# The analysis convolution as 7x7 output blocks with patches as stationary operands, and weight preparation between its products

## The reference

```
x2  = relu(x)                                          # (8,16,56,56)
sub = conv(x2 as (128,1,56,56), f_ana (9,1,9,9), 'SAME')
x3  = concat([sub as 144 channels, x2 (16 channels)])  # (8,56,56,160) tokens
for l, shift in enumerate((0, 3)):
    x3 = x3 + proj(attention(layernorm(x3), windows 7x7, shift))
    x3 = x3 + gelu(layernorm(x3) @ w1 + b1) @ w2 + b2
x3  = x3 @ linw + linb                                 # then a synthesis convolution, a 1x1 convolution
```

## Time and profile before

| what | value |
|---|---|
| median of 3 runs | 3282.6 us (3275.31 to 3290.77) |
| the profiled execution | 3282.26 us, span of its profile 3280.7 us |
| busy, share of the span: PE, PEld | 95%, 86% |
| busy: DVE, ACT, POOL | 67%, 51%, 25% |
| mean granted clock of TensorE | 0.976 |

### The profile page before, as it was taken

The page is one execution under the profiler, slowest core; times in us unless marked ns, Lnnn a source line. Parts: engine busy times, 40 slices in busy tenths (PEclk is TensorE's granted clock), DMA queues, the critical chain, the costliest instruction groups (busy, mean ns, idle before and its releaser), DMA issues. The chain is left out here.

```text
span 3280.7 us, 104199 instructions
## 1 busy us (share of the span) xinstructions
PE 3128.1 (95%) x40530; PEld 2817.2 (86%) x40530; DVE 2190.6 (67%) x6717; ACT 1676.8 (51%) x4073; POOL 832.6 (25%) x1464
## 2 busy tenths in 40 slices
PE   7996999999999999999999999999999999999589
PEld 6784888888888888888888888888888888888589
DVE  1113677777777777777777777777777777777332
ACT  1111566666666666666665555555555556555221
POOL 4400122222222222222222222223232222232110
PEclk9997799999999999999999999999999999999799
DMA  4421011111111111111211111111111111111385
GB/s 88 119 71 51 20 38 37 37 37 37 37 37 37 37 37 37 37 37 37 56 42 39 37 32 36 26 36 37 37 37 31 36 26 37 37 37 26 60 147 89
DMA packets 246679, 148.39 MB, mean 45 GB/s; under 512 B 31729, under 2 KB 246068, under 8 KB 246586
## 3 DMA queue, kind: packets, MB, share of 16 engines
q1 hardware_dynamic: 244882, 146.95, 19.4%
q0 software_dynamic: 1728, 0.48, 0.1%
HBM read 96.74 MB, written 52.50 MB: 45 GB/s over the span
## 5 line engine op out<-in xcount | busy, mean ns | idle before, releaser
L1457 PE MATMUL rm<-w,ht 128*112 128x160 f32 x4480 | 681.0, 301 | 0.0
L1457 PEld LDWEIGHTS rm<-w,ht 128*112 128x112 f32 x4480 | 609.7, 177 | 5.8 <-ACT ht L1034 0.2
L944 POOL TENSOR_TENSOR rs<-ln_tmp,mhalf 112x4 f32<-112x4 f32 (+1 forms) x128 | 119.1, 930 | 1624.4 <-DVE ln_tmp L1116 1624.3
L1034 ACT ACTIVATE ht<-rm 128x448 f32<-128x448 f32 (+1 forms) x640 | 318.6, 498 | 193.8 <-PE rm L118 193.8
L118 PE MATMUL rm<-z2t_hi,w_hi 128*128 128x448 f32 (+1 forms) x640 | 257.5, 402 | 4.8 <-DVE z2t_rest L1226 3.3
L999 ACT ACTIVATE vb<-ra 113x320 f32<-113x320 f32 x256 | 112.9, 441 | 281.1 <-PE ra L118 279.6
L910 POOL TENSOR_TENSOR z<-z,one 112x448 f32<-112x448 f32 (+2 forms) x192 | 131.3, 684 | 354.1 <-DVE z L1120 354.1
L118 PE MATMUL rm<-z2t_rest,w_rest 98*128 98x448 f32 (+1 forms) x640 | 220.0, 344 | 0.0
L118 PE MATMUL rm<-z2t_hi,w_lo 128*128 128x448 f32 (+1 forms) x640 | 219.0, 342 | 0.0
L118 PE MATMUL rm<-z2t_lo,w_hi 128*128 128x448 f32 (+1 forms) x640 | 218.5, 341 | 0.0
L1165 DVE TENSOR_TENSOR sc<-so,tabs 113x490 f32<-113x490 f32 x256 | 171.3, 669 | 59.4 <-PE so L1403 46.9
(11 more groups left out here) (247 smaller groups left out, 9147.6 us busy)
## 6 DMA issues: line engine op xcount, KB each, us to landing
xa<-xs SPq DMA_DIRECT2D x128, 245.0 KB
xr<-xs SPq DMA_DIRECT2D x128, 245.0 KB
xs<-a_tok SPq DMA_DIRECT2D x8, 1960.0 KB, 9.5
xs<-xo SPq DMA_DIRECT2D x64, 245.0 KB
ys<-yz SPq DMA_DIRECT2D x64, 245.0 KB
c_y<-ys SPq DMA_DIRECT2D x48, 260.0 KB
c_y<-ys SPq DMA_DIRECT2D x16, 280.0 KB
c_taps<-in_f_syn SPq DMA_DIRECT2D x24, 126.0 KB, 5.3
```

The source lines that it names most:

```text
L944: gp.tensor_tensor(rs[1][:, t0:t0 + nt], ln_tmp[1][5][:, t0:t0 + nt], mhalf[:, 0:nt], ALU.pow).then_inc(s_pow, 1)
L1034: act_(ht[:, f * SN + t0 * TT:f * SN + (t0 + nt) * TT], bank_m(i, lm, use)[:, 0:nt * TT], ACT.Gelu_apprx_tanh).then_inc(m_freed(i, lm, use ...
L1457: last = mm(bank_m(i, lm, use)[0:TT, t * DIM:(t + 1) * DIM], ht[:, c:c + TT], keep.w["w2", lm][:, f * DIM:(f + 1) * DIM], start=(f == 0), ...
```

## The change

The convolution is laid out anew. The host hands over x padded to 64x64, two images of a pair side by side for each channel, and the filters as one table (`spread_taps`) of 15x15 rows by 490 columns (10 outputs by 7x7 positions, the tenth being the identity). A group `g` is 8 channels of a pair (there are 8 groups). `load_group` brings 128 partitions (8 channels x 2 images x 8 rows of windows) by 15x64 pixels. ScalarE's `relu` cuts them into eight 15x15 patches (`a_win`, 128x1800, one buffer). TensorE turns the patches in four steps `q` (`turn`: 4 transposes of 128x120 or 128x105), ScalarE and VectorE write the high and low parts with patches sorted by channel (`patch_out`, inner stride 8 elements), and for each channel TensorE adds 6 products (2 halves of the 225 patch elements by 3 combinations) in which the patches of 128 windows are the stationary operand and the table of 490 columns moves. That makes 384 products for 64 outputs. `output` copies 128x490 to the token tile, which now holds windows on partitions (inner stride 160 elements), ScalarE the even channels, VectorE the odd ones. The relu is part of the same output.

A pair's tokens are stored by 7 transfers with runs of 1120 elements, when its two groups are through. The last pair's store is issued in `phase_b`, behind its first loads. The token tile of that pair lives on through `phase_b`.

The weight preparation is cut in 13 uses of two PSUM banks (`USES`), one behind every second product of channels from number 26 on (`PREP_AT`). SP issues gains first, then raw weights, and lands each weight's own semaphore, for which GpSimd waits one by one. Bias rows are now the last two rows of `raw_c`, and their split is done by VectorE. The loop over images is unrolled on all engines.

```diff
@@ build
+        with ExitStack() as early:
+            late = LastPair(nc, early, xs0)
+            phase_a(nc, keep, late, x, f_ana, ...)
+            phase_b(nc, keep, late, xs0, xs1, ys)
...
@@ phase_a, sync engine
+            load_group(0)
+            for h in range(2):
+                for oy in range(WIN):
+                    sp.dma_start(view(tok[1], 0, PART[h], h * ON + oy * OXN, [[1, OXN]]),
+                                 dram(f_ana.tensor, (ROW0[h] - oy + WIN - 1) * (PR * OXN), [[OXN, PART[h]], [1, OXN]])
+                                 ).then_inc(s_taps[h], 16)
+            load_group(1)
+            sp.wait_ge(s_win, 1)
+            load_group(2)
...
+            for g in range(3, NG_A + 2):
+                if 3 < g < NG_A:
+                    sp.wait_ge(s_win, g - 1)
+                    load_group(g)
+                pair = (g - 3) // 2
+                if g % 2 == 0 and pair < B // 2 - 1:
+                    for n in range(4):
+                        sp.wait_ge(s_free[n], (pair + 1) * (C // 4))
+                    late.store_pair(sp, pair, tok[pair % 2], s_store[pair % 2])
...
@@ phase_a, scalar engine
+            def relu(g):
+                act.wait_ge(s_nat[g % 2], 16 * (g // 2 + 1))
+                reach(act, s_turn, 4 * g)
+                nc.scalar.activation(view(win, 0, 128, 0, [[PR * PR, WPR], [PR, PR], [1, PR]]),
+                                     view(nat[g % 2], 0, 128, 0, [[WIN, WPR], [PW, PR], [1, PR]]), ACT.Relu).then_inc(s_win, 1)
...
+            for g in range(NG_A):
+                for c in range(0, CG, 2):
+                    n = g * CG + c
+                    output(n)
+                    if g + 1 < NG_A and c < 6:
+                        patch_out(g + 1, c // 2)
+                    if c == 4:
+                        if g + 1 < NG_A:
+                            patch_out(g + 1, 3)
+                        if g + 2 < NG_A:
+                            relu(g + 2)
+                    if PREP_AT.get(n - 2) in ON_ACT:
+                        prep(PREP_AT[n - 2])
...
@@ phase_a, vector engine
+            for g in range(NG_A):
+                for c in range(1, CG, 2):
+                    n = g * CG + c
+                    if g + 1 < NG_A:
+                        patch_out(g + 1, c // 2)
+                    output(n)
...
@@ phase_a, tensor engine
+            def turn(g, q):
+                h, bank = q // 2, turn_ps[q % 2]
+                reach(pe, s_win, g + 1)
+                reach(pe, s_plo, 4 * g + q - 1)
...
+            def conv(g, c):
+                n = g * CG + c
+                if c == 0:
+                    pe.wait_ge(s_plo, 4 * (g + 1))
+                reach(pe, s_free[n % 4], n // 4)
+                cols = slice(c * 128, (c + 1) * 128)
...
+                    for p, b in ((patch_hi, band_hi), (patch_lo, band_hi), (patch_hi, band_lo)):
+                        last = nc.tensor.matmul(conv_ps[n % 4][:, 0:ON], p[g % 2][h][:, cols], b[h][:],
+                                                start=(k == 0), stop=(k == 5))
...
+            for g in range(NG_A):
+                for c in range(CG):
+                    conv(g, c)
+                    if g + 1 < NG_A and c in TURN_AT:
+                        turn(g + 1, TURN_AT.index(c))
+                    if g * CG + c in PREP_AT:
+                        prep(PREP_AT[g * CG + c])
...
@@ phase_b, sync engine
             load(xr, s_xr, 0, 0)
+            late.store_pair(sp, B // 2 - 1, late.tok, late.s_store)
             sp.wait_ge(s_norm[0], 1)
```

More of the change, by code:

```diff
@@ L57 @@
 FT = MLP // 128
-PADF = W - FS // 2 - 1
-FROW = 112
+PR, PW, WPR = WIN + FS - 1, H + FS - 1, W // WIN
+CG = C // 2
+ROW0 = (0, 8)
+PART = (8 * PR, 7 * PR)
+OXN = (K + 1) * WIN
+ON = WIN * OXN
+TURN_AT = [0, 2, 4, 5]
+PREP_FIRST = 26
 ZW = 128 + CR
@@ new lines, in band, with patch_out @@
+            def band(h):
+                act.wait_ge(s_taps[h], 16 * WIN)
+                nc.scalar.activation(band_hi[h][:], taps(h), ACT.Copy).then_inc(s_bhi, 1)
+            def patch_out(g, q):
+                act.wait_ge(s_turn, 4 * g + q + 1)
+                if g >= 2 and q == 0:
+                    last = CG * (g - 1) - 1
+                    act.wait_ge(s_conv[last % 4], last // 4 + 1)
+                nc.scalar.activation(patch(patch_hi, g, q), turned(g, q), ACT.Copy).then_inc(s_phi, 1)
@@ new lines, in output, with prep @@
+            def output(n):
+                act.wait_ge(s_conv[n % 4], n // 4 + 1)
+                tok_room(act, n)
+                nc.scalar.activation(tokens(n), sums(n), ACT.Copy).then_inc(s_free[n % 4], 1)
+            def prep(use):
+                act.wait_ge(s_pfull, USES.index(use) + 1)
+                p = prep_bank(use)
+                if use == "w2T0":
+                    last = nc.scalar.activation(w2t_a[:, 0:4 * 128], p[:, 0:4 * 128], ACT.Copy)
+                elif use == "w2T1":
+                    nc.scalar.activation(w2t_a[:, 4 * 128:MLP], p[:, 0:128], ACT.Copy)
+                    last = nc.scalar.activation(w2t_c[0:REST, 4 * 128:MLP], p[0:REST, 128:256], ACT.Copy)
+                else:
+                    last = nc.scalar.activation(w2t_c[0:REST, 0:4 * 128], p[0:REST, 0:4 * 128], ACT.Copy)
+                last.then_inc(s_pact, 1)
@@ L490, in _ @@
-            body(0, 0)
-            body(0, 1)
-            with dve.Fori(1, B // 2) as pair:
-                for u in range(2):
-                    body(pair, u)
-            n = 0
+            v = nc.vector
+            count = 0
             def step(ins):
-                nonlocal n
-                n += 1
+                nonlocal count
+                count += 1
                 ins.then_inc(s_prep, 1)
-                dve.wait_ge(s_prep, n)
-            dve.wait_ge(s_small, SMALL)
-            dve.wait_ge(s_bps, 1)
@@ L634, in _ @@
-            last.then_inc(s_fold, 1)
-def phase_b(nc, keep, xs0, xs1, ys):
+            def turn(g, q):
+                h, bank = q // 2, turn_ps[q % 2]
+                reach(pe, s_win, g + 1)
+                reach(pe, s_plo, 4 * g + q - 1)
+                for w in range(4):
+                    off = (4 * (q % 2) + w) * PR * PR + ROW0[h] * PR
+                    last = nc.tensor.transpose(bank[0:PART[h], w * 128:(w + 1) * 128], win[:, off:off + PART[h]], keep.ident[:])
+                last.then_inc(s_turn, 1)
@@ L638, in phase_b @@
+            pe.wait_ge(s_pool, 1)
+            for q in range(4):
+                turn(0, q)
+            for g in range(NG_A):
[5 more added lines that the diff above has]
+                        prep(PREP_AT[g * CG + c])
+def phase_b(nc, keep, late, xs0, xs1, ys):
     with ExitStack() as ctx:
```

540 lines of the change are left out of this document (242 added, 298 removed).

## The result

The changed kernel took 3136.3 us in the median of 4 runs (3129.97 to 3140.15), against 3282.2 us (3275.31 to 3290.77) for the kernel before on the same chip. The ratio is 0.9553, with a 95% interval of 0.9538 to 0.9569. The forecast was 3127 us, with a range of 3106 to 3156.

What follows compares the result with a forecast made beforehand. TensorE was taken to bound phase a: 15.2 + 2.0 + 85.2 + 12.2 + 20.1 + 4.2 + 7.2 + 2.0 + 1.3 = 149.4 us, where 303.95 stood. So 3282.3 - 154.6 = 3127.7, say 3127 us; range 3106 to 3156.

Steps and rivals of the forecast that it cites:

- Phase a is TensorE's: Phase a: TensorE as the bound with small stalls, 3115 to 3138 us, given 0.60.
- The products at 0.222 us: Convolution on TensorE: 384 products of 490 columns at 0.222 us each, together 85.2 us.
- Rival (b): Phase a: ScalarE and VectorE set the pace, at 1.4 us per strided operation; 3149 us, chance 0.12.
- Rival (d): Phase a evacuation: slower than before, ScalarE's strided operations 4.2 us each; about 3330 us at 5 us each, chance 0.02.
- The start: Phase a's beginning: loads, relu, transposes and splits put the first product at 15.2 us, where it stood at 9.4.
- The slow stretch behind it: TensorE's first products: some 11 at the lower clock, 0.41 instead of 0.22 us, costing 2.0 us.
- Group bubbles: Between groups: the next group's first product waits for VectorE's low part, 0.6 us in each of 7 groups, 4.2 us.
- That is a wait of 7.2 us: Group 3: TensorE waits 7.2 us for group 4, issued at 58.6 us behind SP's weight list; lower end 1.4 us.
- VectorE's and ScalarE's parts of it are to lie under later products: Weight preparation: these engines' 15.5 us are hidden under products, since groups 3 and 4 stay under TensorE's time.
- The preparation at 20.1 us: Weight preparation on TensorE, moved between products: 20.1 us at full clock, in place of 33.4 us.
- Stores, group 5's load, GpSimd: Phase a: pair stores of 13.9 us and group 5's load all hidden; GpSimd ends near 80 us.
- Its own signs: Profile checks: product spacing 0.22 us, first near 15, one group 3 wait of 1 to 8, phase b loads near 150.

Runs made afterwards that it cites:

- Experiment 4: Changed kernel with output copies written in runs of 7 instead of steps of 160 elements, tokens in wrong order: 3137.0 us, ratio 0.9558.
- Experiment 5: Changed kernel with four products per channel in place of six, leaving out patches' high part with table's low part: 3125.5 us, ratio 0.9526.
- Experiment 1: Changed kernel with the loads of groups 4 and 5 issued among the raw weights, not behind all weights: 3134.6 us, ratio 0.9551.
- Experiment 2: Changed kernel with ScalarE's weight preparation ahead of the patches and relu of the same step, not behind them: 3131.8 us, ratio 0.9543.
- experiment 3: Changed kernel with all weight preparation behind the last product of the convolution, as before the change: 3144.6 us, ratio 0.9586.
- experiment 6: Changed kernel with the last pair's store issued and waited for in phase a, ahead of phase b's loads: 3150.1 us, ratio 0.9599.
- experiment 9: The changed kernel itself, unchanged, run again in a later sitting: 3139.4 us, ratio 0.9566.
- 8: Experiment 7's kernel with pair 0's store issued right behind group 5's load and preparation from product 36 on: 3127.0 us, ratio 0.9532.
- experiment 7: Changed kernel with groups 4 and 5 loaded among raw weights, ScalarE's preparation ahead of its patches, preparation from product 30 on: 3120.1 us, ratio 0.9507.

## Why the prediction was right, and what it missed

**Phase a is TensorE's.** The products at 0.222 us held to the digit, and so did 0.41 us at the lower level of the clock. Rival (b) wanted 1.4 us for each strided operation, and none shows more than 1.18. Experiment 4 adds that with outputs at 0.58 us the kernel is no faster. Experiment 5 says how near the chain over ScalarE and VectorE was: of 3.55 us less in a group's products 1.3 turned into waiting. Rival (d) would have wanted four times the price that the rows show.

**The start** was put at 15.2 us and is 16.05. The slow stretch behind it was put at 2.0 us, and group 0 takes 15.28 us to the next group's first product where the others take 13.15, so 2.1 more.

**Group bubbles** were put at 0.6 us in each of 7 groups, 4.2 us, and measured 0.25 to 0.48 where they occur, 2.1 us in all. That the patches cost 1.18 us and not 1.05 did not show. Against that a group's own work took 12.7 us, not 12.4. Each change from transposes to products costs about 0.1 us, which the sum had not. The two about cancel.

**"That is a wait of 7.2 us"** is the mis-sized term. It measured 10.13: TensorE came 1.7 us later than said (59.24), and the relu ended 4.6 us later (69.31). The forecast issued group 4 at 58.6 us, and it was at 62.82. SP began with the weights 0.5 us later than said (9.56), and 3.7 us lie in the list itself, which took 52.7 us beside group 3's load where the earlier trace rows gave 49.0. It has single issues of 2.55, 2.00 and 4.26 us, as the list before had of other sizes. By comparison with their like the held issues come to some 9.0 us here, where the prediction counted 5.8 before. Why they were held no run shows. The prediction counted such held issues as possible savings at the lower end, and not as a cost that could grow. Experiment 1 confirms the cause: with the load moved up, the wait is gone. The wait's length isn't firm either. The same list ended in the other runs such that group 4 was issued between 62.23 and 65.58 us.

**"VectorE's and ScalarE's parts of it are to lie under later products"** is the step that failed. VectorE's part did lie there. The engines' busy times left room for ScalarE's too, and the order on ScalarE did not. A bank was freed 1.8 us late, and the low clock behind it took about 3.4 us more (7.94 us at 0.57). Experiment 2 removed both, 5.7 us. The prediction compared sums of busy time by group, and had not followed the queue of one engine at the places where another waits for it.

**The preparation at 20.1 us** was about right. Behind the load, experiment 3 needs 63.7 us to the end of its products (70.29 to 133.99), and 65.3 with the 1.6 us from there to phase b's first load that the forecast has; experiment 2 needs 84.2 with the preparation in between, so it costs 18.9 us there.

**Stores, group 5's load, GpSimd** were hidden as said (GpSimd ended at 88.2 us rather than 80), and experiment 6 gave the price of a bare store, 14.8 us where 13.9 was estimated. **Phase b** was unchanged within its spread, by experiment 9.

**Its own signs** held but for two: the wait in group 3 was to be 1 to 8 us, and phase b's first loads were to stand near 150 us. The two errors of phase a add up, and the total stayed in the range because it was wide enough for both.

The excess of 4.7 + 4.9 = 9.6 us over the forecast is thus mostly the queue, which issued the load 4.2 us late, and ScalarE's order. In experiment 1 the missing weights took back 5.9 us, and the held cast at most the 1.0 us by which the wait at 102.96 is longer.

## What to carry to other kernels

When one engine sets the pace, the loss lies in the few places where it waits for something that another engine or queue has put behind unrelated work. Look there for order, and not only for busy time. A wait of some 2 to 3 us on TensorE cost 1.5 to 3 times its length here, since products ran at half clock behind it, for 3 to 10 us. Moving a load or a store forward pays only until the next item in the same queue is the late one: here 10.1 us of wait removed gave 3.4 us, until the consumer was moved back as well.

## What the runs showed of the hardware

- A copy from PSUM of 490 elements costs ScalarE 582 ns when it writes in runs of 7, and 1065 ns with single elements 640 bytes apart; VectorE 660 and 1056 ns. A stride of 32 bytes costs about as much as one of 640 (1180 ns for 512 elements).
- The Trainium skill ("SBUF — State Buffer", section "Door 1: The DMA port swizzle") has lines of 16 bytes and a penalty for each access that goes to a new one, by which both strides pay alike. The trace agrees, with 2.30 and 2.17 ns for an element.
- Casts on VectorE beside GpSimd's row of twenty table additions were either held until 0.3 us behind the row's end (4.30 us for 2x640 elements in experiment 1, 4.31 and 2.78 us for 2x480 in experiments 6 and 8) or hardly at all (0.45 to 0.69 us for 2x480 in the changed kernel, in its second execution and in experiments 2 and 4). The row took 6.7 us in the first case and 7.6 us in the second. Without the row such casts took 0.49 and 0.41 us.
- Products of 490 columns stood 0.222 us apart. The 207 ns of the Trainium skill ("TensorE: Matmul & The Clock Gate", section "Wait — 56ns, not 53.3ns?") were not reached, as they were not at 448 columns.
- A low clock followed waits of TensorE of 1.82, 2.35, 2.51, 2.65, 3.07 and 10.13 us. It did not follow those of 1.65, 1.51 and 1.47 us in experiment 5 (a granted clock of 1.00 behind each), but in the same run it followed one of 1.67 us at 143.18 (0.50 from 145 to 147 us), and in experiment 7 two of 0.76 and 0.89 us within 1.6 us. The length of the last wait alone doesn't tell.
